# Score operands of a decoder layer: another order of their channels in DRAM, larger pieces in their loads, four buffers for split q and k

## The reference

```python
x = _layernorm(x + _L0_attn_ref(x, w_qkv, w_proj, b_proj, rel_bias_table))   # self-attention, relative position bias
x = _layernorm(x + _L0_xattn_ref(x, ctx_1024, ctx_1024))                     # attention to ctx, no projections
x = _layernorm(x + _L0_ffn_ref(x, centroids, ln_g, ln_b, w1, b1, w2, b2))    # each token by one of 8 experts
```

## Time and profile before

| | us |
|---|---|
| median of 3 runs | 1129.08 (1123.93 to 1131.08) |
| the profiled execution | 1131.16 |
| its span, first to last instruction | 1129.3 |
| PE busy | 972.1 (86%) |
| ACT busy | 771.5 (68%) |
| DVE busy | 667.4 (59%) |
| DMA moved | 162.92 MB |

### The profile page before, as it was taken

The page is one execution under the profiler, slowest core; times in us unless marked ns, Lnnn a source line. Parts: engine busy times, 40 slices in busy tenths (PEclk is TensorE's granted clock), DMA queues, the critical chain, the costliest instruction groups (busy, mean ns, idle before and its releaser), DMA issues. The chain is left out here.

```text
span 1129.3 us, 17448 instructions
## 1 busy us (share of the span) xinstructions
PE 972.1 (86%) x5213; PEld 514.7 (46%) x5213; DVE 667.4 (59%) x1762; ACT 771.5 (68%) x1456; POOL 319.6 (28%) x311
## 2 busy tenths in 40 slices
PE   7089999998989899999999999996089888898891
PEld 2023333333433343333333333333089878898790
DVE  4056766666767677734444555465357766686672
ACT  2067767676767677889888987892068777767770
POOL 2021030211111111100220221021314666666664
PEclk8589998989899998999999998996589998898995
DMA  7968877768685957679668965740143433343351
GB/s 226 166 244 134 191 179 173 181 160 203 134 228 108 243 105 176 114 148 258 114 119 127 166 123 88 129 94 20 51 165 112 164 102 111 118 152 120 108 178 41
DMA packets 93728, 162.92 MB, mean 144 GB/s; under 512 B 18447, under 2 KB 41806, under 8 KB 89742
## 3 DMA queue, kind: packets, MB, share of 16 engines
q1 hardware_dynamic: 88592, 152.78, 57.7%
q0 software_dynamic: 5056, 9.20, 2.9%
HBM read 116.41 MB, written 49.54 MB: 147 GB/s over the span
## 5 line engine op out<-in xcount | busy, mean ns | idle before, releaser
L693 ACT ACTIVATE probs<-sc 128x512 f32<-128x512 f32 x1024 | 528.9, 608 | 136.7 <-DVE sc L778 102.0
L474 PE MATMUL sc<-qst,kst 57*128 57x512 f32 (+1 forms) x1024 | 272.0, 482 | 37.9 <-ACT probs L693 21.8
L778 DVE TENSOR_TENSOR sc<-sc,strip 128x308 f32<-128x308 f32 (+1 forms) x512 | 193.6, 430 | 98.5 <-PE sc L474 96.6
L474 PEld LDWEIGHTS sc<-qst,kst 57*128 57x128 f32 (+1 forms) x1024 | 120.8, 190 | 230.2 <-ACT probs L693 181.8
L486 PE MATMUL ot<-probs,vals 128*32 128x512 f32 x1600 | 224.2, 634 | 0.0
L1694 POOL DMA_INDIRECT f_rows<-s_x,f_get_ids x45 | 106.4, 2365 | 36.1 <-issue 24.3
L507 PE MATMUL ms<-xT,w_qkv 128*128 128x512 f32 x128 | 68.7, 666 | 22.3 <-DMA xT<-in_xT 19.4
L1552 ACT ACTIVATE f_h<-f_h_ps,f_par 128x384 f32<-128x384 f32 x104 | 64.3, 619 | 25.5 <-PE f_h_ps L1471 25.4
L1632 DVE TENSOR_TENSOR f_h_lo<-f_h,f_h_hi 128x384 fp32r<-128x384 f32 x104 | 56.9, 547 | 27.3 <-ACT f_h_hi L1553 26.9
L1170 POOL TENSOR_SCALAR veps<-mv_self 128x4 f32<-128x4 f32 x8 | 1.9, 232 | 229.3 <-DVE mv_self L836 229.3
L1553 ACT ACTIVATE f_h_hi<-f_h_ps,f_par 128x384 fp32r<-128x384 f32 x104 | 64.7, 622 | 0.0
(11 more groups left out here) (155 smaller groups left out, 1578.9 us busy)
## 6 DMA issues: line engine op xcount, KB each, us to landing
s_qk<-split SPq DMA_DIRECT2D x32, 512.0 KB, 4.8
strip<-in_w_all SPq DMA_DIRECT2D x16, 1024.0 KB, 12.6
f_raw<-in_w_all SPq DMA_DIRECT2D x14, 1024.0 KB
kst<-s_qk SPq DMA_DIRECT2D x96, 128.0 KB, 4.3
qst<-s_qk SPq DMA_DIRECT2D x96, 128.0 KB, 6.9
kst<-s_ctx_parts SPq DMA_DIRECT2D x96, 128.0 KB, 6.6
qst<-s_x_parts SPq DMA_DIRECT2D x96, 128.0 KB, 8.4
s_x_parts<-split SPq DMA_DIRECT2D x16, 512.0 KB, 8.8
```

The lines of the kernel that those rows point to most:

```text
L474: nc.tensor.matmul(sc[j][:], kst[at:at + rows, i, P * c:P * c + P], qst[at:at + rows, i, :], start=True, stop=True).then_inc(scored, 1)
L693: nc.scalar.activation(probs[:, k % KEPT, j, :], sc[j][:], ACT.Exp, scale=scale).then_inc(exped, 1)
L778: nc.vector.tensor_tensor(sc[j][:, lo:hi], sc[j][:, lo:hi], band_backwards(rank_of(4 * g + j), at, hi - lo), ALU.add).then_inc(biased, 1)
```

## The change

The channels of a pair are put in the order half, dimension, slot, where they were slot, half, dimension. It is done on the host, by the order of the columns of w_qkv, w_proj, b_proj, x and ctxT (`mixed_channels`); `x1` keeps that order, and the residual of the cross-attention (L858) reads it back in the old one. In DRAM the four slots of a dimension now follow one another, so that a partition of `kst` or `qst` is filled by one piece of 8 KB. The high and low part, or the high part twice, of one half go in one DMA of 32 partitions, and the third 16 rows in another: 8 DMAs a pair. `parts` moves to `w_hi0` and gets four buffers, each with a semaphore for its store.

```diff
+def mixed_channels():
+    return np.arange(C).reshape(PAIRS, SLOTS // PAIRS, 2, D).transpose(0, 2, 3, 1).reshape(C)
...
-        parts, xparts = [four[:, 0], four[:, 1]], [four[:, 2], four[:, 3]]
+        spare = w_hi0.rearrange("p m (i s n) -> p (m i) s n", s=2, n=N)
+        parts, xparts = [spare[:, i] for i in range(4)], [four[:, 2], four[:, 3]]
...
-        st_parts = [sem("st_q"), sem("st_k")]
+        st_parts = [sem(f"st_parts{i}") for i in range(4)]
...
-        PAIR_LOADS = 12 * 16
+        PAIR_LOADS = 8 * 16
...
-                             parts[i % 2].bitcast(F32)).then_inc(st_parts[i % 2], 16)
+                             parts[i].bitcast(F32)).then_inc(st_parts[i], 16)
...
-                    for s in st_parts:
-                        wait(sp, s, 16 * (2 * n + pair + 1))
+                    for s in st_parts[2 * pair:2 * pair + 2]:
+                        sp.wait_ge(s, 16 * (n + 1))
...
-                for src, dst, order in ((k_from, kst, (0, 1, 0)), (q_from, qst, (0, 0, 1))):
-                    for r, part in enumerate(order):
-                        two = src[part, P * pair:P * pair + P].rearrange("(i s d) n -> s d i n", s=2, d=D)
-                        for half in range(2):
-                            row = HALF * half + D * r
-                            sp.dma_start(dst[row:row + D, some, :].bitcast(F32), two[half]).then_inc(ld_pair[pair], 16)
+                for half in range(2):
+                    for src, dst in ((k_from, kst), (q_from, qst)):
+                        row, at = HALF * half, P * pair + HALF * half
+                        each = src[:, at:at + HALF].rearrange("t (d s) n -> t d (s n)", d=D)
+                        two = each if dst is kst else bass.AP(each.tensor, each[0].offset, [[0, 2], *each[0].ap])
+                        sp.dma_start(dst[row:row + 2 * D, some, :].bitcast(F32), two).then_inc(ld_pair[pair], 16)
+                        sp.dma_start(dst[row + 2 * D:row + 3 * D, some, :].bitcast(F32), each[0 if dst is kst else 1]).then_inc(ld_pair[pair], 16)
...
-                wait(act, st_parts[i % 2], 16 * (2 * b + i // 2))
-                nc.scalar.activation(parts[i % 2][:, 0, :], ms[i % 2][:], ACT.Copy).then_inc(qk_hi, 1)
+                wait(act, st_parts[i], 16 * b)
+                nc.scalar.activation(parts[i][:, 0, :], ms[i % 2][:], ACT.Copy).then_inc(qk_hi, 1)
...
-                    cols = slice(C // G * g, C // G * (g + 1))
-                    last = nc.vector.tensor_tensor(xr[:, t, cols].rearrange("p (h d) -> p h d", d=D),
...
+                    cols, some = slice(C // G * g, C // G * (g + 1)), slice(2 * (g % 2), 2 * (g % 2) + 2)
+                    last = nc.vector.tensor_tensor(xr[:, t, cols].rearrange("p (s h d) -> p s h d", h=2, d=D),
+                                                   ms[t % 2][:, pair].rearrange("p (s h f) -> p s h f", s=2, f=32)[:, :, :, at:at + D],
+                                                   x1_in[:, t, pair].rearrange("p (h d s) -> p s h d", h=2, d=D)[:, some], ALU.add)
...
                     dve.wait_ge(ld_w0, 32)
+                    for s in st_parts:
+                        dve.wait_ge(s, 16 * B)
```

More of the change, by code:

```diff
@@ L812, in low_qk @@
                 dve.wait_ge(qk_hi, 4 * b + i + 1)
-                nc.vector.tensor_tensor(parts[i % 2][:, 1, :], ms[i % 2][:], parts[i % 2][:, 0, :].bitcast(F32),
+                nc.vector.tensor_tensor(parts[i][:, 1, :], ms[i % 2][:], parts[i][:, 0, :].bitcast(F32),
                                         ALU.subtract).then_inc(qk_lo, 1)
@@ L854, in add_x2 @@
                 for g in range(G):
-                    at = P * (g // 2) + D * (g % 2)
-                    cols = slice(C // G * g, C // G * (g + 1))
-                    last = nc.vector.tensor_tensor(xr[:, t, cols].rearrange("p (h d) -> p h d", d=D),
-                                                   ms[t % 2][:, P * (g // 2):P * (g // 2) + P].rearrange("p (h f) -> p h f", f=32)[:, :, at % P:at % P + D],
-                                                   x1_in[:, t, cols].rearrange("p (h d) -> p h d", d=D), ALU.add)
+                    at, pair = D * (g % 2), slice(P * (g // 2), P * (g // 2) + P)
+                    cols, some = slice(C // G * g, C // G * (g + 1)), slice(2 * (g % 2), 2 * (g % 2) + 2)
+                    last = nc.vector.tensor_tensor(xr[:, t, cols].rearrange("p (s h d) -> p s h d", h=2, d=D),
+                                                   ms[t % 2][:, pair].rearrange("p (s h f) -> p s h f", s=2, f=32)[:, :, :, at:at + D],
+                                                   x1_in[:, t, pair].rearrange("p (h d s) -> p s h d", h=2, d=D)[:, some], ALU.add)
                 last.then_inc(added, 1)
@@ L1784, in lay_out @@
     chunks = lambda v: v.reshape(E, -1, P).transpose(0, 2, 1)
-    ranked = sorted(range(H), key=rank_of)
+    ranked, mixed = sorted(range(H), key=rank_of), mixed_channels()
     w1 = a["L0_ffn_w1"].transpose(0, 2, 1).reshape(E, DC, P, F).transpose(0, 2, 1, 3).reshape(E, P, W_COLS)
@@ L1788, in lay_out @@
     return dict(
-        x=a["x"], ctx=a["ctx_1024"], xT=a["x"].transpose(0, 2, 1), ctxT=a["ctx_1024"].transpose(0, 2, 1),
-        w_qkvT=a["L0_attn_w_qkv"].T, w_projT=w_proj.reshape(PAIRS, P, C), b_proj=a["L0_attn_b_proj"],
+        x=a["x"][..., mixed], ctx=a["ctx_1024"], xT=a["x"].transpose(0, 2, 1), ctxT=a["ctx_1024"].transpose(0, 2, 1)[:, mixed],
+        w_qkvT=a["L0_attn_w_qkv"].T[:, np.concatenate([mixed, C + mixed, np.arange(2 * C, 3 * C)])], w_projT=w_proj.reshape(PAIRS, P, C)[..., mixed], b_proj=a["L0_attn_b_proj"][mixed],
         table=a["L0_attn_rel_bias_table"][:, ranked], centroidsT=a["L0_ffn_centroids"].T, w_all=np.stack([w1, w2], axis=2),
```

## The result

The change makes the kernel slower: **1389.28 us** (median of 4 runs, 1386.26 to 1390.38) beside 1130.08 for the kernel before on the same chip, a ratio of 1.2298 (95% interval 1.2257 to 1.2340). The forecast was 1276 in a range of 1195 to 1365: the sign and the place are right, the size is short by 113 us. The profiled execution took 1389.14 us with a span of 1387.3, 258 us more than the span of before, and the mean granted clock went from 0.915 to 0.837.

A forecast was written before the change was run, and what follows sets the result against it. Self-attention was taken as bound by PE plus some 4 us a pass, cross-attention by PE alone. With large loads on two engines, +37, +7, +76, +8 and +19 made +147, so 1276 us, range 1195 to 1365.

The forecast's parts named there:

- (a): Load issues on SyncE: four fewer a pair save 1.85 us a pair, worth something only in the start.
- (b): Copy of the high half: four buffers remove its 5.75 us store wait, 23 us over passes 2 to 6 unless loads bind.
- (d): 256 KB loads: t (2) outermost confines them to two fixed engines, 4.9 us each; main case, chance 0.78.
- the choice for `far` as the nearest row: Large-load price taken from `far` into `qst` (twice 8 rows of 16 KB), read as leaving some engines without work.
- The rivals that spread it or hid it partly: Loads spread over 16 engines: 1097 us, chance 0.13; two engines partly differing between loads: 1202 us, chance 0.05.
- (c): 128 KB loads: one 8 KB piece an engine, 0.31 us each, 1.2 us for the four of a pair.
- The rest of a cross pass: Cross passes, 48 us forecast: DMA traffic besides the pair loads, 1.62 MB, takes 4.1 us an engine.
- gaps: Each self or cross pass: 2 us added for loads issued only after the pair's scores and landing late.
- The start: Before the passes: first pair fills two engines until 46, delaying stores, second pair, `earlier` and xT; +19 us.
- Pass 7, pass 15: Pass 7 takes 53 us, +7; in the middle of pass 15 the second pair's load lands at 759, +8.
- The bound of 65 for a self pass: Upper bounds: self pass 65 us, cross pass 54, start +28, the rest +22, together +235.
- the bounds of nothing and twice: Residual read in steps of four: 128 instructions of 218 ns cost between nothing and twice that extra; 0 taken.

The follow-up runs named there:

- d_outer_two: The d_outer kernel with the two buffers of the kernel before for split q and k: 1115.61 us, ratio 0.9890.
- d_outer: The changed kernel with d (16) outermost and t (2) inside it in the 256 KB loads, same bytes and pieces: 1091.01 us, ratio 0.9664.
- twelve: The changed kernel with twelve loads of 16 partitions a pair, as in the kernel before, but in pieces of 8 KB: 1108.00 us, ratio 0.9851.
- no_small: The changed kernel without the 128 KB loads, so only the 256 KB loads remain: 1298.19 us in one run.
- start_early: The d_outer kernel with `earlier` and xT of the next sequence issued ahead of the second pair's loads: 1077.31 us, ratio 0.9561.
- four_buffers: The kernel before with the four buffers for split q and k alone, loads and channel order untouched: 1097.57 us, ratio 0.9722.

## Why the prediction was wrong in size

**(a) Instructions.** The step put their worth in the start alone. d_outer_two shows them and the wider loads together at 12 us, and none of it in the start: pass 1 begins at 104.0 (104.2 before), and 5 of the 12 us are in passes 1 to 6.

**(b) Buffers.** Right. The copy's wait is gone in the changed kernel, and by itself the edit takes 29 us from passes 2 to 6 (from 273.1 to 244, at the mean of 48.8 each) where the step had 23. That it would come to nothing behind slow loads is what happened.

**(d) The large load.** Right, and the choice for `far` as the nearest row with it: two engines, the same two in every load, since the share stays at 0.12 to 0.13 in stretches 20 us apart with several loads queued. At 26 GB/s an engine the 4.9 us a load hold. The rivals that spread it or hid it partly are excluded by these rows, and d_outer shows that the order of two dimensions is the whole cause: it turns a ratio of 1.23 into 0.97. One reading in the step was wrong, without harm. It took the share of 0.34 (37.0 to 38.5 us, kernel before) for 5.4 engines. Two more windows of that kernel:
```profile
34.00:35.00 1.00, 0.00 (x0) 0.00 (x0) 0.00 (x0) 0.00 (x0) 0.00 (x0) 0.50 1.61 252
38.50:41.00 2.50, 0.97 (x4) 0.50 (x4) 0.00 (x0) 0.00 (x0) 0.00 (x0) 0.50 0.49 175
```
No more than all of the engines can be busy, so a share of 1.61 isn't a count of them: the view books the whole time of a piece in the window in which it starts, and the 16 KB pieces of `far` run on for up to 1.97 us. So 0.34 is too low for the pieces still under way. Behind them the share is 0.49, eight engines, as many as `far` has outer rows; that was the row to read.

**(c) The small load: here the forecast failed.** The step put it at "one piece, 0.31 us at that rate; four a pair are 1.2 us", with the rate of a transfer over 128 partitions. The same step names 162 GB/s, all engines busy, for loads of 16 partitions, and puts that down to pieces of 2 KB. twelve shows that it isn't the piece: 16 partitions filled by pieces of 8 KB get 122 to 142 GB/s. And no_small measures the term: 0.80 us in self passes, near the 0.81 of 128 KB at 162 GB/s, and 0.59 in cross passes, where 0.31 was put. Put in, that is 3.9 us more a self pass: 60 becomes 63.9, measured 63.8. Over the six passes that is 23 us, and 22.5 were missing (59.5 less 37).

Why a small load costs the two engines more than their own piece was not tested. The pass at 759.5 has a stretch with four small loads, and one with nothing but large ones:
```profile
759.80:764.80 5.00, 5.00 (x24) 1.12 (x22) 0.00 (x0) 3.51 (x7) 1.92 (x2) 0.50 0.49 114
792.50:807.00 14.50, 14.50 (x100) 6.19 (x96) 3.70 (x8) 12.18 (x24) 1.00 (x3) 0.99 0.13 53
```
A busy engine moves 14.5 GB/s in the first (114 over 0.49 of 16) and 25.5 in the second. The other fourteen engines have 14 pieces of each small load, 459 KB of the 570 KB moved in the first stretch. That leaves 111 KB for the two, where 5 us at 53 GB/s are 265: by this estimate the large loads lose 2.9 us while the small ones are written, 0.7 us each, with the two engines' own pieces still to come. It is one stretch, and more than no_small's 0.59, so the 0.81 above may agree by chance.

**The rest of a cross pass.** Here 48 was forecast and 55.7 measured. The small loads explain 2.3 of the 7.7 us (4.8 less the 2.5 that the step has for eight). The other 5.4 aren't the small loads, since no_small takes 51.0 a cross pass where 48 less 2.5 is forecast. The trace of pass 759.5 to 813.8 puts them at the mixed slices: 27 slices with the large loads alone take 36.7 us (1.85 MB at 53 GB/s is 34.9; the 1.8 us over it are near the 2 put for gaps, though no slice has a share under 0.1), the other 13 slices take 17.7 us and hold 0.25 MB of large loads (4.7 us), eight small ones (4.8 at no_small's price) and the rest, 1.52 MB. That leaves 8.2 us for the rest, where the step had 4.1 at 24.5 GB/s an engine. With the 2.3 of the small loads these 4.1 make up the 6.3 us that this pass of 54.3 has over 48; the mean of the seven is 1.4 us longer still. This is read from one pass and wasn't tested by a run; the packets under 2 KB (1734 of 2123) speak for small pieces as its reason, without proving it. In self passes the rest isn't off like this: no_small takes 57.4 a pass, and 60 less 2.5 is forecast. Why it costs double in cross passes alone stays open.

**The start.** +19 was forecast, +39.6 came up to the start of pass 1. The stations: second pair issued at 55.84 (forecast 51), DVE released at 85.36 (74), PE at 90.46 (79):
```profile
21.77 0.75 SPq L303 DMA_DIRECT2D kst<-s_qk  x1
...
27.06 8.20 SPq L283 DMA_DIRECT2D s_qk<-w_hi  x2
...
55.84 0.62 SPq L303 DMA_DIRECT2D kst<-s_qk  x1
...
65.44 8.80 SPq L340 DMA_DIRECT2D ctxT<-in_ctxT  x1
...
81.47 0.43 SPq L462 DMA_DIRECT2D xT<-in_xT  x1
```
```profile
53.55 1.22 PE L482 MATMUL sc<-qst,kst 57*128 57x512 f32 x4 [26.41 <-DMA qst<-s_far]
...
90.46 3.78 PE L515 MATMUL ms<-xT,w_qkv 128*128 128x512 f32 x4 [35.69 <-DMA xT<-in_xT]
...
143.85 1.22 PE L482 MATMUL sc<-qst,kst 57*128 57x512 f32 x4 [8.71 <-issue]
```
(SP's queue, then PE.) Three issues keep SyncE for 8.2 us (two stores), 8.8 and, a little later, 5.8 (`w_out`), where the same issues took 0.89, 0.51 and 0.47 in the kernel before: I read it as the issue itself waiting for room behind two engines' full queues, which no run took apart, and xT is issued only at 81.47. The forecast let DMAs land late, but had every issue at its old pace. The 11 us at PE's station are read. Of the remaining 10 of pass 0, 8.7 are PE's idle time right ahead of pass 1, the last row. The profile names no releaser for it; the loads of the pair that comes next were issued from 113.30 on, 30.5 us before. The step for the start has no term for this wait. start_early shows the other side, with the loads spread: what stands ahead of `earlier` and xT in that queue is worth 13.4 us of pass 0.

**Pass 7, pass 15.** +13.6 and +12.2 for +7 and +8. I put this down to the same terms, one pass each; it wasn't followed up.

**The sum.** Misses of 21 (start), 22.5 (passes 1 to 6), 6.6 (7), 54.5 (8 to 14), 4.2 (15) and 2.6 (after) are 111. Of these the small load accounts for 24 + 16 in passes 1 to 14 but 7 and, by no_small's 91 less 40 us, for 51 in all. The range ended at +235 over the kernel before, and +258 came. The bound of 65 for a self pass held (63.8); that of 54 for a cross pass (55.7), of +28 for the start (39.6) and of +22 for the rest (28.4) didn't. None of the three had a price for a slower small load, though its own row, 162 GB/s, stood in the text.

**L866** (L858 before) takes 257 ns instead of 218, 18% more, within the bounds of nothing and twice; DVE is busy for a third of the cross passes and hides it.

## What to carry to other kernels

Write out the pattern of a DMA and look at its outermost dimension first: here the loop over t ahead of d left two engines of 16 with all the work, and swapping the two gave 298 us for one line. A DMA share of 2/16 with PE waiting for a load is the sign of it, and the engines' rate is then of no concern. And price a transfer by a row that has its partition count: the small load, taken from a transfer over 128 partitions, cost more of the forecast than any other term.

## What the runs showed that wasn't expected

- With all 16 engines shown busy, loads into 16 partitions move 122 to 142 GB/s with pieces of 8 KB (twelve) and 144 with 2 KB (four_buffers); those into 32 partitions, mixed with the small ones, 172 and 177 (d_outer); those into 128 partitions 426. The size of the pieces makes no difference to the first two, then; the number of partitions goes with the rate, but so does the size of the DMA (128 KB the first, 256 KB the second), which no run varied by itself.
- The issue of a store of split q or k on SyncE took 0.36 to 0.54 us in the kernel before and up to 10.5 us in the changed one, where two engines carried all large loads; everything behind it on SyncE waited too. In each of the passes 1 to 6 at least one took 3.9 us or more.
